# Order of the values' product and of the next group's keys and queries, in an attention and mixture-of-experts kernel

## What is computed

```
q = (layernorm(x) @ Wq + bq)   k = (ctx @ Wk + bk)   v = (ctx @ Wv + bv)      # 64 sequences x 128 tokens x 256
attn = softmax(q k^T / sqrt(16)) v                                            # 16 heads of 16
x = x + attn @ Wo + bo
router softmax over 8 experts, the best 2 of each token, their two weights normalised
x = x + sum over the 2 experts of  w_e * ( silu(xn @ gating_e) * (xn @ up_e) ) @ down_e,   xn = layernorm(x)
```

## Time and profile before

| | us |
|---|---|
| median of 3 runs | 1359.26 (1358.9 to 1364.22) |
| the profiled execution | 1358.88, its span 1357.1 |
| TensorE busy | 1300.3 (96%) |
| VectorE busy | 673.5 (50%) |
| ScalarE busy | 725.4 (53%) |
| GpSimd busy | 423.9 (31%) |
| chain that ended last | TensorE 57%, VectorE 2% |

### The profile page before, as it was taken

How to read it: one execution, slowest core, us unless ns; L and a number is a source line. 1 busy time by engine, 2 the same in 40 slices (tenths; PEclk the granted TensorE clock), 3 DMA queues, 4 the chain that set the end, 5 groups by cost and what they waited for, 6 DMA issues and landing times.

```text
span 1357.1 us, 37763 instructions
## 1 busy us (share of the span) xinstructions
PE 1300.3 (96%) x13790; PEld 1122.3 (83%) x13791; DVE 673.5 (50%) x1974; ACT 725.4 (53%) x1106; POOL 423.9 (31%) x353
## 2 busy tenths in 40 slices
PE   6999999999999999889999999999999999999996
PEld 3777676676667667679999999999999999999996
DVE  3667776777777776744454333333333333333332
ACT  3566656666666665566654444444444444444443
POOL 3112223333333333214454322222222222222222
PEclk9999999999999999999999999999999999999999
DMA  4434444444444433214343333333333323233332
GB/s 140 118 112 118 128 131 133 134 137 141 140 129 136 124 111 95 74 44 82 76 84 76 51 48 47 47 51 47 48 50 47 47 47 51 47 48 49 47 47 35
DMA packets 98716, 112.52 MB, mean 83 GB/s; under 512 B 13072, under 2 KB 85776, under 8 KB 98608
## 3 DMA queue, kind: packets, MB, share of 16 engines
q1 hardware_dynamic: 71120, 72.87, 19.3%
q0 software_dynamic: 26400, 37.09, 16.1%
q10 hardware_dynamic: 1088, 1.05, 0.2%
HBM read 48.72 MB, written 45.46 MB: 69 GB/s over the span
## 4 chain that ended last, share of the span: by engine, by line
PE 57%; DVE 2%; DMA 1%; issue 1%; POOL 1%; ACT 0%; DVEq 0%; POOLq 0%; ACTq 0%
PE banks L477 53%; PE banks L681 2%; DMA out<-x_sb,token 1%; DVE row_max L985 1%; POOL sorted_x L400 1%; PE banks L520 0%; PE banks L506 0%; PE banks L532 0%; DMA sorted_x<-xn,slots_now 0%; PE banks L543 0%; DVE attn L1001 0%; PE banks L569 0%; DVE x L1006 0%; POOL out L430 0%; PE banks L549 0%
## 5 line engine op out<-in xcount | busy, mean ns | idle before, releaser
L430 POOL DMA_INDIRECT out<-x_sb,token x135 | 210.2, 1557 | 495.4 <-DVE x_sb L1259 426.4
L1246 DVE TENSOR_TENSOR qT<-qT,banks 128x512 f32<-128x512 f32 x135 | 92.8, 687 | 437.0 <-PE banks L477 437.0
L843 ACT ACTIVATE qT<-banks 128x512 f32<-128x512 f32 x135 | 80.6, 597 | 365.3 <-PE banks L477 365.1
L477 PE MATMUL banks<-xnT,kT 128*128 128x128 f32 x2176 | 265.3, 275 | 0.0
L477 PE MATMUL banks<-xnT,probs 128*128 128x128 f32 x2144 | 261.6, 275 | 0.8 <-DVE xnT L1241 0.8
L477 PEld LDWEIGHTS banks<-xnT,kT 128*128 128x128 f32 x2176 | 258.7, 192 | 3.8 <-issue 0.4
L477 PEld LDWEIGHTS banks<-xnT,probs 128*128 128x128 f32 x2144 | 254.7, 192 | 4.7 <-DVE xnT L1241 1.2
L477 PE MATMUL banks<-down_sb,qT 128*128 x1080 | 255.6, 380 | 0.8 <-DVE x_sb L1259 0.8
L477 PEld LDWEIGHTS banks<-down_sb,qT 128*128 128x128 f32 x1080 | 194.9, 191 | 22.0 <-issue 1.2
L400 POOL DMA_INDIRECT sorted_x<-xn,slots_now x128 | 124.5, 972 | 182.6 <-DVE slots_now L1075 122.0
L985 DVE TENSOR_REDUCE row_max<-banks 128x16 f32<-128x2048 f32 x64 | 146.7, 2292 | 67.8 <-PE banks L506 65.2
(11 more groups left out here) (161 smaller groups left out, 1665.2 us busy)
## 6 DMA issues: line engine op xcount, KB each, us to landing
xn<-sorted_x SPq DMA_DIRECT2D x136, 130.5 KB
x_sb<-in_x SPq DMA_DIRECT2D x16, 512.0 KB, 3.9
ctxT_sb<-in_ctx SPq DMA_DIRECT2D x16, 512.0 KB, 4.1
heads<-kT SPq DMA_DIRECT2D x128, 64.0 KB, 2.4
heads<-qT SPq DMA_DIRECT2D x128, 64.0 KB, 2.3
out<-x SPq DMA_DIRECT2D x16, 512.0 KB
gate_sb<-_L_ffn_kernel_gating_EDF SPq DMA_DIRECT2D x8, 512.0 KB, 4.7
up_sb<-in_L_ffn_kernel_up_EDF SPq DMA_DIRECT2D x8, 512.0 KB, 4.5
```

Of the source, the lines that this page charges most:

```text
L430: pool.indirect_dma_start(out=out[:, :], out_offset=bass.IndirectOffsetOnAxis(ap=token[:, v, :], axis=0), in_=ys[:, u, :], in_offset=None, ...
L477: last = nc.tensor.matmul(dst, lhsT, rhs, start=(i == 0), stop=(i == len(pairs) - 1))
L843: nc.scalar.activation(gatedT[:, u, :], score[:, u, :], ACT.Silu).then_inc(s_silu, 1)
L1246: nc.vector.tensor_tensor(fusedT[:, u, :], gatedT[:, u, :], score[:, 2 + u, :], ALU.mult).then_inc(s_fuse, 1)
```

## The change

For b = 0, 1 and 2 the two products of bank 1 trade places. The values of sequence i + 1 are made ahead of `attend`, and the piece of keys or queries behind `swap_back`; the wait between them is now for the copy of the values (`s_vc`). ScalarE's copies trade places likewise: the values are copied right behind `attT`, and the piece stands behind the second half of the first norm (b = 0) or the second norm (b = 2). For b = 3 the order is as before. In the last group there is no next group, and the values alone stand ahead of `attend`. No instruction is added or removed.

```diff
@@ TensorE, stage_a
                     wait(pe, s_exp, i * 3 - 1)
-                    if nxt:
-                        if b < 2:
-                            keys(g + 1, 1 - u, b, other_bank(i, 1))
-                        else:
-                            queries(g + 1, b - 2, other_bank(i, 1))
+                    if b < 3:
+                        values(u, b + 1, other_bank(i, 1))
+                    elif nxt:
+                        queries(g + 1, 1, other_bank(i, 1))
                     if one:
                         attend(i - 1, (b + 1) % 2, other_bank(i, 2))
                     swap_max(i, other_bank(i, 3))
...
                     if one:
                         swap_back(i - 1, other_bank(i, 2))
-                    if b < 3 or nxt:
+                    if nxt and b < 3:
+                        wait(pe, s_vc, i + 2)
+                        if b < 2:
+                            keys(g + 1, 1 - u, b, other_bank(i, 1))
+                        else:
+                            queries(g + 1, 0, other_bank(i, 1))
+                    if nxt and b == 3:
                         wait(pe, s_piece_c, min(5 + i, SEQS))
-                        values(u if b < 3 else 1 - u, (b + 1) % GROUP, other_bank(i, 1))
+                        values(1 - u, 0, other_bank(i, 1))
@@ ScalarE, stage_a
-                    if nxt:
-                        copy_piece(g + 1, 1 - u, b, other_bank(i, 1))
+                    if nxt and b == 3:
+                        copy_piece(g + 1, 1 - u, 3, other_bank(i, 1))
                     if one:
                         copy_attT(i - 1, other_bank(i, 2))
+                    if b < 3:
+                        copy_values(i + 1, (b + 1) % 2, other_bank(i, 1))
...
-                    if b < 3 or nxt:
-                        copy_values(i + 1, (b + 1) % 2, other_bank(i, 1))
+                    if nxt and b < 3:
+                        copy_piece(g + 1, 1 - u, b, other_bank(i, 1))
+                    if nxt and b == 3:
+                        copy_values(i + 1, 0, other_bank(i, 1))
```

## The result

The changed kernel's median over 20 executions is 1356.19 us (19 of them from 1353.2 to 1360.2), that of the kernel before 1363.28 in the 20 executions measured beside it. One execution of the changed kernel took 2658.1 us at full clock, for a reason that is open, and is left out of the ratio and of what follows. The ratio is **0.9952**, its 95% interval 0.9938 to 0.9965: faster by half a per cent, where 0.76% had been forecast (1348.6 against 1358.9). The profiled execution of the kernel before (1358.88), from which the forecast was reckoned, was among its quickest; that of the kernel after, 1360.20, is the longest of the 19. So the two traces differ by +1.4 us in span, and have to be read piece by piece. In the lines of after, VectorE's have moved by nine and ScalarE's by five.

The account below looks back on a forecast made before the run. TensorE's own work plus two waits at b = 2, for the second norm and `attn`, was taken to bound groups 3 to 14. Order -4.2 and clock -6.1 made -10.3: 1358.9 to 1348.6 us, range 1345 to 1358.

Parts of the forecast that it names:

- The chain: VectorE at b = 0, GpSimd, VectorE, ScalarE set when TensorE goes on at b = 2; it comes 0.62 us earlier.
- the new idle time: TensorE waits at the swaps of b = 0, 1, 2 and at `places`; idle time per group 2.10 becomes 1.48 us.
- The gaps at the three swaps: TensorE waits for the maxima at b = 0, 1, 2: 0.34 + 0.25 + 0.57 = 1.16 us a group.
- the wait at `places`: At b = 2 TensorE waits 0.32 us for `attn`, and `places` starts 0.62 us earlier than before.
- The price of the values: Ahead of the swap, values take 0.86 us start to start in place of a piece's 1.82.
- late behind the values' copy: Sign of a wrong forecast: ScalarE's second norm at b = 2 late; forecast to end at 328.0 with 0.6 us to spare.
- -4.2 us by the order: Whole kernel without the clock: -7.4 us from groups 3 to 14 and +3.2 from the first groups.
- Groups 3 to 14 have this chain: 12 x -0.62: Each of groups 3 to 14 gets 0.62 us shorter, -7.4 us together.
- The first groups' +3.2: Group 0 loses 2 us or a little more, group 1 pays 1.2, group 2 is even: +3.2 us.
- I take it that the falls go: Clock falls in groups 3, 4, 5 and 13, 1.52 us each, disappear: -6.1 us.
- The falls stay: Rival, chance 0.20: the clock falls in some groups for a reason other than these waits; 1354.7 us.
- The chain doesn't come forward: Rival, chance 0.11: groups stay as long, first groups' +3.2 stand; 1362.1 us with the falls, 1356.0 without.
- More falls: Rival, chance 0.10: clock falls behind the new gaps, once in each of groups 0 to 14, +22.8 us: 1371.

Follow-up runs that it names:

- b0_only: Changed order (values ahead of `attend`) at b = 0 alone, b = 1 and 2 as in the kernel before: 1353.05 us, ratio 0.993.
- b12_only: Changed order (values ahead of `attend`) at b = 1 and 2 alone, b = 0 as in the kernel before: 1357.82 us, ratio 0.9967.
- keep2_before: Kernel before, with GpSimd's `keep_x` made to wait until the routing step `gap` is done: 1349.34 us, ratio 0.9887.
- table_after: Changed kernel, with VectorE's adds of `tiles_to` in group 14 moved from b = 1 to b = 2: 1350.31 us, ratio 0.9907.
- scalar_adds: Changed kernel, with `n_tiles` as the scalar operand in the adds of `tiles_to` instead of a second tensor: 1351.31 us, ratio 0.9919.
- b0_late_table: Kernel before, with the changed order at b = 0 of groups 3 to 15 alone and group 14's adds of `tiles_to` at b = 2: 1349.79 us, ratio 0.9902.
- keep_b0: b0_late_table, with GpSimd's `keep_x` made to wait for `route_third` of group g - 2 (CHOSEN): 1392.61 us, ratio 1.0208.

## Why the prediction was right in its chain and wrong in its size

**The chain: right.** That b = 0 starts it, and that only b = 0 matters, is shown by `b0_only` and `b12_only`; that `keep_x` beside the shift is its link, by `keep2_before`. The gain of a group was put at 0.62 and measured 0.65. The sum of the new idle time was right and its division was not. The gaps at the three swaps were put at 0.34, 0.25 and 0.57 and the wait at `places` at 0.32, 1.48 together. Measured in group 8, from the start of `attend` to the swap less the 1.01 that this takes without a gap, they are 0.19 (1.20), 0.03 (1.04) and 0.28 (1.29); at `places` it is 0.95 (325.88 - 324.49 - 0.44). That makes 1.45, and 2.10 - 1.45 is the 0.65 by which the group is shorter. The price of the values was read at their place behind the swap back, 0.86. Ahead of `attend` they take 1.00, 1.06 and 0.97 from start to start, and the piece, in the values' place, takes 1.72 where it took 1.82 to 1.91. So the swaps give up less idle time, TensorE reaches `x1_swapped` earlier than reckoned, and stands at `places` instead, where the trace has 0.79 and not 0.2 to 0.3. The norm did not get late behind the values' copy, and no wait for `attT` or the exponentials showed.

**The sum.** The forecast was -4.2 us by the order and -6.1 by the clock, -10.3 together. Measured are -4.3 at equal clock and -2.8 by the clock, -7.1 together. That the first of the two terms fits is luck: it hides a stall that costs 2.5 and a term for the first groups that was too high.

**The step that failed** is "Groups 3 to 14 have this chain: 12 x -0.62". Group 14 has it too, but also VectorE's adds, which no other group has, and I had read none of the rows of that place. The change pulls GpSimd forward by 0.6 us in every group and puts those adds 0.4 later; before, they ended 0.21 ahead of it. The question "what is late next" was asked of TensorE and ScalarE, and not of what VectorE does in the same moment as the engine that now comes earlier. It cost 3.4 us by the trace (11.99 against the 8.56 of `table_after`), 2.5 at equal clock, and in the profiled execution a double fall besides. Without it the ratio is 0.9907, more than the forecast of 1348.6 / 1358.9 = 0.9924.

**The first groups' +3.2** came out to the tenth in the ledger, and for another reason. The first swap came 1.3 later, and a clock fall stood at 22 to 29. In `table_after` and `scalar_adds`, where the fall of the start is over before the first swap, groups 0 to 2 take 99.88 and 99.89 us from swap to swap, and in the kernel before 98.84: +1.0, or +1.7 if the 0.66 by which the swap of group 3 comes forward is counted back. So the term was put two to three times too high, and with the stall gone the whole order wins 6.8 at equal clock instead of 4.2. `b0_late_table` and `keep2_before` have the later start and a fall too (23 to 27), with those groups' code as it was. Why the program's start differs so is open.

**"I take it that the falls go"** was half right. In groups 3, 4 and 5 they went, and they went with b = 0 changed (`keep_b0` apart) or with `keep_x` held back behind `gap`, the edits that shorten the waits of b = 2, and in part stayed with `b12_only`, which doesn't. But others appeared, at the start, behind the count (513), in groups 14 and 15 and in stage B, and the 6.1 us were not won: in the profiled execution the clock's loss went from 6.8 to 13.7, and the median clock only from 0.989 to 0.992. Four falls had been taken as a fixed number, and it is one that changes from one execution to the next. The fall at 537 stands behind the stall and is absent without it, but `b0_only` has a stall of 2.83 at the same place and no fall; the cause of this fall and of those at 513, 578 and 592 stays open.

**The rivals.** "The falls stay" gives 1354.7, 4.2 below the base, and at equal clock the measured kernel is 4.3 below; but that agreement is made of 6.8 won without the stall, and 2.5 lost in it. "The chain doesn't come forward" is out by the 0.65 a group. "More falls" behind the new small gaps is out too: groups 6 to 12 have them at each of three swaps and a clock at full. The rule of the Trainium skill that was held against the change ("TensorE: Matmul & The Clock Gate", section "A second HAM failure mode: psum-queue depth-cycling") is not borne out here by gaps of 0.03 to 0.3 us.

## What to carry over

When a change pulls one engine's work forward, look in every iteration, the odd ones too, at what the other engines do at the new moment: one stall of 3.6 us in one group of sixteen took over a third of the gain at equal clock (2.5 of 6.8). A wait on TensorE whose named releaser was long ready should be followed back until an operation stands there with a duration that its size doesn't explain (1.79 us for 128x4), since removing that cause (one wait on GpSimd, -1.1%) was worth more than reordering around it (-0.5%, and -0.9% with the stall gone; at equal clock 9.8 us against 4.3 and 6.8). And where the granted clock falls at random, compare kernels at equal mean clock before arguing from one trace.

## What the hardware showed

- VectorE with two tensors in SBUF can be held up beside an operation of GpSimd until that ends, however small its own work: beside `keep_x`, `gap` (128x4) took 2.29 in place of 0.15 and the shift 1.79 or 1.03 in place of 0.15, and one add of 128x1 that began in `root2` took 3.04 in place of 0.16. Two such adds just before it ran beside the start of `root2` unhindered, and so did a step with two tensors beside the scatters. With one operand as a column of scalars the adds took 0.21 each, with one operand in PSUM an add beside `keep_x` its usual 0.42.
- A wait *added* to GpSimd made the kernel 1.8% slower at one semaphore value and 1.1% faster two routing steps later.
- The clock falls came in two lengths here, 1.7 and 3.4 us lost, and differ between executions of one kernel by up to 0.012 of mean clock, 12 us.
